# A gated cross-attention and mixture-of-experts layer: the second norm's split rows turned by TensorE and copied by VectorE, in place of DMA transposes

## What is computed

```python
x = x + tanh(g_xattn[0]) * attention(layernorm(x), ctx)      # 8 heads of 64, softmax, Wo, bias bo
h = layernorm(x)
logits = einsum('bnd,de->bne', h, gate_w)                    # 8 experts
topv, topi = top_k(logits, 2); w = softmax(topv)
u, v = h @ Wu[e], h @ Wv[e]; Y = (silu(u) * v) @ Wo[e]       # for the two chosen experts
x = x + tanh(g_ffn[0]) * sum_k(w_k * Y_k)
```

## Time and profile before

| | us |
|---|---|
| median of 3 runs | 1104.78 |
| lowest, highest | 1104.33, 1106.05 |
| the profiled execution | 1094.02 |
| its span, first to last instruction | 1092.3 |
| TensorE busy | 895.8 (82%) |
| VectorE busy | 679.3 (62%) |
| ScalarE busy | 570.6 (52%) |
| GpSimd busy | 537.8 (49%) |

### The profile page before, as it was taken

One profiled execution on the slowest core, in us unless ns is written; L12 is line 12 of the kernel. 1 busy time (PEld: TensorE's weight loads), 2 busy tenths in 40 slices (PEclk: granted clock), 3 DMA queues, 4 the chain that ended last, 5 costly groups with the idle time before them and its releaser, 6 DMA issues.

```text
span 1092.3 us, 22761 instructions
## 1 busy us (share of the span) xinstructions
PE 895.8 (82%) x8210; PEld 543.4 (50%) x8210; DVE 679.3 (62%) x1595; ACT 570.6 (52%) x1022; POOL 537.8 (49%) x645
## 2 busy tenths in 40 slices
PE   4888878998899899899889889997540999799880
PEld 2344435555455455545545545554320787577660
DVE  5687757677677767767776786676424554344440
ACT  3367646567456556655765665565220564555450
POOL 6122234253466447456545644546663246556564
PEclk9999989999999999999999999998965899999995
DMA  7555773422372264345226425635343589889996
GB/s 269 151 166 157 232 252 78 138 71 74 84 210 67 59 189 111 70 132 160 73 69 198 102 66 174 185 91 162 101 151 125 134 184 192 169 186 192 192 150 81
DMA packets 125757, 154.26 MB, mean 141 GB/s; under 512 B 48336, under 2 KB 81104, under 8 KB 124880
## 3 DMA queue, kind: packets, MB, share of 16 engines
q1 hardware_dynamic: 108784, 115.40, 36.4%
q0 software_dynamic: 16864, 37.40, 17.9%
HBM read 62.83 MB, written 56.30 MB: 109 GB/s over the span
## 4 chain that ended last, share of the span: by engine, by line
PE 49%; DMA 13%; DVE 13%; issue 9%; ACT 8%; POOL 5%; SPq 2%; POOLq 1%; ACTq 0%; DVEq 0%
PE G L1239 25%; DMA out_dram<-V,Ph 10%; PE ST L1295 4%; PE ST L1296 4%; PE MX L1281 3%; PE G L1248 3%; PE MX L1463 2%; DVE mx L879 2%; PE PV L1310 2%; PE PV L1308 2%; POOL out_dram L668 2%; PE PV L1312 2%; DVE tiles L869 2%; POOL expert_rows L582 1%; PE G L1455 1%
## 5 line engine op out<-in xcount | busy, mean ns | idle before, releaser
L625 POOL TENSOR_TENSOR Pl<-P,Ph 128x512 f16<-128x512 f32 x128 | 152.4, 1195 | 222.7 <-ACT Ph L703 222.2
L700 ACT ACTIVATE P<-ST 128x512 f32<-128x512 f32 x256 | 153.3, 599 | 207.7 <-PE ST L1296 178.6
L879 DVE TENSOR_REDUCE mx<-MX 128x1 f32<-128x512 f32 x256 | 168.1, 683 | 26.9 <-PE MX L1281 26.8
L703 ACT ACTIVATE Ph<-ST 128x512 f16<-128x512 f32 x256 | 154.6, 604 | 0.3
L668 POOL DMA_INDIRECT out_dram<-V,Ph x78 | 122.1, 1566 | 46.0 <-ACT V L836 28.1
L1463 PE MATMUL MX<-heads,tiles 128*128 128x256 f16 x936 | 119.0, 279 | 19.3 <-DVE heads L1193 18.9
L1308 PE MATMUL PV<-V,Ph 128*128 128x65 f16 x1024 | 113.1, 194 | 15.8 <-issue 15.7
L1310 PE MATMUL PV<-V,Ph 128*128 128x64 f16 x1024 | 113.5, 196 | 3.1 <-issue 3.1
L1308 PEld LDWEIGHTS PV<-V,Ph 128*128 128x128 f16 x1024 | 97.0, 98 | 36.6 <-issue 19.1
L1312 PE MATMUL PV<-V,Pl 128*128 128x65 f16 x1024 | 113.1, 194 | 1.9 <-issue 1.9
L1463 PEld LDWEIGHTS MX<-heads,tiles 128*128 x936 | 90.9, 100 | 41.6 <-issue 24.5
(11 more groups left out here) (206 smaller groups left out, 1912.6 us busy)
## 6 DMA issues: line engine op xcount, KB each, us to landing
heads<-expert_rows SPq DMA_DIRECT2D x39, 516.0 KB
tiles<-in_x_dram SPq DMA_DIRECT2D x32, 256.0 KB, 4.8
tiles<-in_ctx_dram SPq DMA_DIRECT2D x32, 256.0 KB, 5.1
second_norm<-in_x_dram SPq DMA_DIRECT2D x32, 256.0 KB, 2.9
out_dram<-second_norm SPq DMA_DIRECT2D x32, 256.0 KB, 2.3
heads<-q_hi SPq DMA_DIRECT2D x124, 64.0 KB
heads<-k_hi SPq DMA_DIRECT2D x124, 64.0 KB
expert_rows<-second_norm SPq DMA_DIRECT2D x2, 2064.0 KB, 11.1
```

The lines of the kernel that those rows point to most:

```text
L625: nc.gpsimd.tensor_tensor(Pl[:, hh, c, :], P32[:, c, :], Ph[:, hh, c, :], ALU.subtract).then_inc(pl_pool, 1)
L700: nc.scalar.activation(P32[:, c, :], ST[:, c % 2, :], ACT.Exp, scale=0.125 / SC2).then_inc(p_ready, 1)
L703: nc.scalar.activation(Ph[:, hh, c, :], ST[:, c % 2, :], ACT.Exp, scale=0.125 / SC2).then_inc(ph_ready, 1)
L879: nc.vector.tensor_reduce(out=mx[:, k // TT, k % TT:k % TT + 1], in_=MX[:, (k + odd) % 2, :], axis=AXX, op=ALU.max).then_inc(mx_taken, 1)
```

## The change

The function turn moves from SyncE to TensorE. It waits for the row split, takes a use of the general bank (named x2T), seen as 1024 f16 columns, and turns the eight 128x128 blocks of both parts into it with the f16 identity. VectorE copies the whole bank to x2T in SBUF (take_turned), and logits wait for that copy. Both happen in step n + 6. Where logits stood, turn now stands; logits follow the transposes of oT and of the maxima. On VectorE the copy takes the place of take_logits, which moves behind oT_lo and ahead of best_two. In the closing rounds turn stands between oT and out.

```diff
         if g >= 6:
-            names.append(("logits", g - 6))
+            names.append(("x2T", g - 6))
         if b:
             names.append(("oT", g - 4))
+        if g >= 6:
+            names.append(("logits", g - 6))
         first, second = side(g)
...
-            def turn(n):
-
-                k = n % 2
-                sp.wait_ge(row_split, n + 1)
-                if n == 0:
-                    sp.wait_ge(prefix_st, K * 16)
-                if n >= 2:
-                    sp.wait_ge(filled, use["logits", n - 2] + 1)
-                for a in range(2):
-                    sp.dma_start_transpose(x2T[:, k, a], row_part(n, a)).then_inc(x2_turned[k], 16)
...
+            def take_turned(n):
+                dve.wait_ge(filled, use["x2T", n] + 1)
+                if n == 0:
+                    dve.wait_ge(prefix_st, K * 16)
+                nc.vector.tensor_copy(x2T[:, n % 2].rearrange("p c n -> p (c n)"),
+                                      bank(("x2T", n)).bitcast(F16)).then_inc(evacuated, 1)
...
                 if g >= 6:
-                    take_logits(g - 6)
+                    take_turned(g - 6)
                 if nmax:
                     max_rows(mxn + 8, odd)
+                if b:
+                    lo_part(("oT", g - 4), oT[1][:], oT[0][:], 1.0)
+                if g >= 6:
+                    take_logits(g - 6)
                 if j == 1 and b >= 2:
                     best_two(b - 2)
-                if b:
-                    lo_part(("oT", g - 4), oT[1][:], oT[0][:], 1.0)
...
+            def turn(n):
+
+                g = bank(("x2T", n)).bitcast(F16)
+                pe.wait_ge(row_split, n + 1)
+                for a in range(2):
+                    for c in range(KC):
+                        last = nc.tensor.transpose(g[:, (a * KC + c) * P:(a * KC + c + 1) * P],
+                                                   row_part(n, a)[:, c * P:(c + 1) * P], C["ident16"][:])
+                last.then_inc(filled, 1)
+
             def logits(n):
                 g = bank(("logits", n))
                 k = n % 2
-                pe.wait_ge(x2_turned[k], (n // 2 + 1) * 32)
+                pe.wait_ge(evacuated, use["x2T", n] + 1)
...
             for g in range(STEPS, STEPS + 6):
                 if g < STEPS + 4:
                     transposes(("oT", g - 4), O[(B - 1) % 2][:, g - STEPS, :])
+                turn(g - 6)
+                if g < STEPS + 4:
                     out_project(g - 4)
                 logits(g - 6)
```

More of the change, by code:

```diff
@@ L87, in bank_uses @@
         if g < steps + 4:
-            names += [("oT", g - 4), ("out", g - 4)]
+            names.append(("oT", g - 4))
+        names.append(("x2T", g - 6))
+        if g < steps + 4:
+            names.append(("out", g - 4))
         names.append(("logits", g - 6))
@@ L171, in layer @@
         xn2 = take(2 * D).bitcast(F32)
-        x2T = take(4 * D).rearrange("p (k a c n) -> p k a c n", k=2, a=2, c=KC)
+        x2T = take(4 * D).rearrange("p (k c n) -> p k c n", k=2, c=2 * KC)
         spare_native = second[:, RING * ROW + 4 * D:RING * ROW + 8 * D].rearrange("p (n a s) -> p n a s", n=2, a=2)
@@ L302, in layer @@
         row_split = sem("xn2_row_split")
-        x2_turned = [sem(f"xn2_turned{k}") for k in range(2)]
         gw_ld = sem("gate_w_loaded")
@@ L485, in step @@
                     clear_blank_rows()
-                if g >= 5:
-                    turn(g - 5)
                 if j == 2 and b < B - 2:
@@ L1325, in logits @@
                 k = n % 2
-                pe.wait_ge(x2_turned[k], (n // 2 + 1) * 32)
-                parts = [(x2T[:, k, a, c, :], Wg[m][:, c, :]) for c in range(KC) for a, m in PASSES + ((1, 1),)]
+                pe.wait_ge(evacuated, use["x2T", n] + 1)
+                parts = [(x2T[:, k, a * KC + c, :], Wg[m][:, c, :]) for c in range(KC) for a, m in PASSES + ((1, 1),)]
                 product(g[:, 0:E], parts).then_inc(filled, 1)
@@ L1409, in step @@
                 if g >= 6:
-                    logits(g - 6)
+                    turn(g - 6)
                 if b:
@@ L1415, in step @@
                     max_transpose(g + 1)
+                if g >= 6:
+                    logits(g - 6)
                 scores(b, j, 5)
```

## The result

The changed kernel took 1116.2 us (median of six runs, 1111.6 to 1119.5), the kernel before 1102.7 (six runs, 1096.7 to 1106.1; three of them are those of the table above): ratio 1.0118, interval 1.0088 to 1.0147, so 13.5 us slower. The prediction had the direction and, as it turned out, most of the mechanism, but 24.4 us for the size and a range that began at 1119. The two profiled executions make the difference look larger, 25.5 us: the one of before is shorter than all six runs (1094.0), the one of after is the longest of its six (1119.5). Two further comparisons of the same pair gave 1.0129 (1.0094 to 1.0164) and 1.0228 (1.0198 to 1.0259). The last is 24.6 us. Why the same change costs 13.5 us on one chip and 24.6 on another is what this part is about.

A forecast was written before the change was run, and what follows sets the result against it. TensorE, almost without a pause, was taken to bound the kernel. Body costs of 29.8 us less 5.4 at the end gave 24.4, added to the profiled 1094.0 plus 10.8 for timed runs: 1129 us, range 1119 to 1136.

The forecast's parts named there:

- Kinds 2 and 3, the bank's order: Third and fourth steps of a batch: V must wait for oT_lo, costing 11.5 and 8.3 us over six steps each.
- The step that failed: Attention steps: TensorE almost never pauses, so anything added to its path lengthens the step; no size of its own.
- the sum: All terms together: the body 29.8 us slower, the end 5.4 us faster, 24.4 us slower net.
- SyncE's transposes in the body: Attention steps: removing DMA transposes frees SyncE, which mostly waits for q_lo there, so it gains nothing.
- Kind 0: First step of a batch: one set of four transposes follows another after oT_lo, 0.45 us a step, 2.3 in five.
- Kind 1: Second step of a batch: read-outs of xn and context follow best_two, 0.9 us a step, 4.5 in five.
- Last batch: Steps 28 to 31, without side tiles: moved logits, later best_two and the copy cost 3.2 us, between 0.5 and 4.
- The end: Closing rounds: without DMA transposes, earlier scatters and a shorter last row save 5.4 us, between 2 and 6.5.
- The last row: Closing rounds: from the last split to logits' read-out 2.4 to 2.5 us instead of 4.5, saving 2.0 us.
- the scatters: Closing rounds: GpSimd's scatters, bound by places and row 29's split, start near 795.6 instead of 799.01, saving 3.4 us.
- Rival (d): First and second steps and last batch give their cost back as waits shift: 14.4 us slower, 1119 us; chance 0.09.
- The Trainium skill's 390 ns: TensorE's transposes: this price would make eight cost 3.1 us, near 1199 us in all; the trace's 0.056 us each was preferred.

The follow-up runs named there:

- w1: The kernel before, with TensorE also waiting for oT_lo's read-out ahead of the first V product in a batch's third and fourth steps: ratio 1.0177.
- e5: The kernel before, DMA transposes kept, with only logits moved behind oT's transposes, in the bank's order and on both engines: 1117.6 us, ratio 1.031.
- e3: The changed kernel with the 64 DMA transposes put back as dead work: ratio 1.0237 on a chip without pauses, 1.0121 on one with.
- e4: The kernel before without DMA transposes, logits fed with unturned rows: ratio 0.9973 on a chip without pauses, 0.9960 on one with.
- f2: The kernel before without DMA transposes, logits fed unturned rows and moved behind the out product in all but each batch's second step: ratio 0.9985.
- h2: The changed kernel, logits behind the first V product in kinds 2 and 3, oT_hi between the norms in kinds 0 and 1: ratios 1.0089, 1.0056.

## Why the prediction was wrong, point by point

- **Kinds 2 and 3, the bank's order** (1.91 and 1.39 us a step): right as a cost against the kernel without pauses: 26.25 - 24.35 = 1.90, and 24.12 - 22.4 to 22.6 = 1.5 to 1.7. w1 measured it by itself, e5 showed that transposes and copy add nothing.
- **The step that failed** is the one ahead of all sums: TensorE "almost without a pause", so that "what is added to its path there is added to the step". The ten pauses of 0.25 to 1.13 us behind V in the profile before were part of that path, and in the changed kernel, whose new wait comes earlier in the same steps, they are gone: most of the cost took their place instead of adding to them. Measured on the chips that pause, kind 2 grew by 0.6 to 1.3 us in steps 18, 22 and 26, kind 3 by 0.4 to 0.9 us in steps 19, 23 and 27. The twelve steps together grew by 11.3 us between the first two profiles and by 13.0 between those of chip B, where the sum had 19.8. Step 6, without scatters and pauses, grew by 1.92.
- **Kind 3's late k_lo** took the same way: in the kernel before it ends 10.95 to 12.2 us after a step's start, which moved V; in the changed kernel V waits for oT_lo in any case, and steps are even at 24.12. So step 7 grew by 0.78 in the first pair, where k_lo had ended at 12.09, and by 1.86 on chip B, where it had ended at 11.00.
- **SyncE's transposes in the body, costed at nothing**: right as far as the runs tell, against my own first theory after the result (e3 and e4 on both sorts of chip).
- **Kind 0** (0.45): 21.27 - 20.83 = 0.44. **Kind 1** (0.9): 23.37 - 22.89 = 0.48; best_two took 1.8 us in its new place (566.71 to 568.53), not 2.2.
- **Last batch** (3.2 us): too low. From the start of step 28 to that of step 31 the changed kernel took 61.0, 58.5 and 58.8 us (first comparison, chips B and C), the kernel before 53.7, 54.1 and 53.6 (first comparison, B and D): 4 to 7 us, so this term was mis-sized. With a granted clock of 1.00 in both, steps 28 and 29 took 18.99 and 20.95 us on chip B, against 17.84 and 18.98 before. Half-clock stretches came on top in the profile after (20.82 and 22.64); the window 734 to 738 us of step 28 (PEclk, DMA share, GB/s at its end):

```profile
734.00:738.00 4.00, 4.00 (x50) 2.57 (x48) 2.38 (x6) 2.66 (x5) 1.35 (x2) 0.67 0.42 102
```

- **The end** (-5.4): from step 31's start to the end of the span 339.6 became 336.0, -3.6 us. The last row was right (from its split's end at 847.49 to the read-out of logits at 850.14 2.65 us, where 2.5 was said); the scatters were not, since row 29's split, not the places, released them: they begin 45.1 us after step 31's start instead of 46.3, 1.1 us won instead of 3.4.
- **The sum against the profiles**: steps 6 to 27 grew by 16.4 us (first pair) and 17.6 (chip B) where the sum had 26.6, the last batch by 7.3 and 4.4 where it had 3.2, the end by -3.6 and -2.7 where it had -5.4: together 20.1 and 19.3 us, against 13.5 and 15.2 of the timed runs. The clock is part of the difference: on chip B the profiled executions lost 57.6 us (before) and 60.0 (changed) to it, as time times the share not granted, an estimate, but the timed runs 64.8 and 61.8. The remainder is not located.
- **Rival (d)**, 1119 us, was nearest on the chips that pause, but for the wrong reason: kinds 0 and 1 and the last batch paid. On chip C, without pauses, the forecast of 24.4 us met 24.6 partly by luck, as the last batch and the end were off in the same direction and the clock gave some 1.8 us of it back (65.3 us lost against 63.5, estimated in the same way).
- The Trainium skill's 390 ns for a transpose of 128x128 (VectorE: DVE Perf Modes, The three transpose paths) is not what a train of them costs here: seven or eight lie some 0.06 us apart at full clock. The trace decides, as the prediction had it.

No kernel tried beats the kernel before. Only e4 and f2 lie below it, by 0.3 to 0.4% and by 0.15% (not clear of noise), and both leave the turning of the rows out. h2 keeps TensorE's transposes at 0.7% less than the changed kernel on a chip that pauses and 1.4% less on one that doesn't, still 0.6% and 0.9% above before.

## What to carry to other kernels

A wait added to the engine that sets the time can cost less than its length where idle time stands later in the same stretch: 0.6 to 1.3 us instead of 1.9 here. Before adding a cost up, compare the lengths of steps of the same kind in the profile; where they differ with the same program (25.65 and 24.95 us here), find the gaps with no releaser and ask whether the new wait comes ahead of them.

A ratio measured on one chip can be of that chip: here the same two programs differ by 1.2 to 1.3% or by 2.3%. To price one edit, prefer the lengths of single steps, which mostly agreed to 0.02 us from chip to chip in the kernels that had the wait, falls of the clock apart.

## What the runs showed that I had not expected

TensorE paused inside trains of matmuls that follow each other every 0.03 us, 0.2 to 1.4 us at a time, in steps in which GpSimd scatters rows, in three of the six comparisons and never in the three others, which ran on two chips (in the last of them only kernels with an added wait were profiled). The granted clock was 1.00 in each pause. The window around e4's pause of 1.18 us on a pausing chip, and the same place of the same program on the other:

```profile
579.52:581.52 2.00, 1.07 (x15) 0.80 (x16) 0.88 (x2) 0.87 (x2) 0.97 (x1) 1.00 0.92 248
```
```profile
575.60:577.60 2.00, 2.00 (x11) 0.93 (x10) 0.95 (x4) 0.31 (x1) 2.00 (x2) 1.00 0.91 318
```

TensorE works 1.07 us of the one and all of the other, with the DMA engines as busy (0.92 and 0.91). All pauses of kinds 2 and 3 lie beside the scatters or within 0.8 us behind one, and steps 6 and 7 have neither. What TensorE lacks in a pause stays open: the trace shows no releaser. The queue that brings instructions in pieces of 16 KB (69 to 71 in a run, a median of some 1.1 us each) took as long in profiles with pauses as in those without, and at most two of the 10 to 16 pauses of a profile overlap one of its transfers. The scatters' own packets had the same median, some 0.17 us, in all profiles. Open too is why a wait ahead of V keeps the pauses away.
